# Selective scan: three of sixteen products with C on GpSimd, B's product for both halves at once, step sizes summed by TensorE, B's rows broadcast by DMA

## What is computed

```python
dt = softplus(einsum('btr,ir->bti', dt_lo, dt_proj_w) + dt_proj_b)
def step(h, inp):
    dt_t, B_t, C_t, x_t = inp
    dA = exp(dt_t[..., None] * A[None])
    dBx = dt_t[..., None] * B_t[:, None, :] * x_t[..., None]
    h = dA * h + dBx
    y_t = sum(h * C_t[:, None, :], axis=-1)
...
y = (y + Dp * xc) * silu(z)
return einsum('bti,di->bd', y, out_proj_w)
```

## Time and profile before

| | us |
|---|---|
| median of three runs | 4557.76 |
| the profiled execution | 4557.68 |
| its span, first to last instruction | 4555.9 |
| first scan instruction starts | 1192.81 |
| last product with C starts | 2063.63 |
| last copy of the stage (`take_sum`) starts | 2070.63 |

### The profile page before, as it was taken

How to read it: one execution, slowest core, us unless ns; L and a number is a source line. 1 busy time by engine, 2 the same in 40 slices (tenths; PEclk the granted TensorE clock), 3 DMA queues, 4 the chain that set the end, 5 groups by cost and what they waited for, 6 DMA issues and landing times. The chain is left out here.

```text
span 4555.9 us, 92840 instructions
## 1 busy us (share of the span) xinstructions
PE 3902.2 (86%) x30083; PEld 1984.7 (44%) x30084; DVE 3239.7 (71%) x7596; ACT 2951.3 (65%) x5997; POOL 2373.4 (52%) x2953
## 2 busy tenths in 40 slices
PE   7599999899677777779879999996988699997897
PEld 4244444463222222226423333335984244443896
DVE  3588888448799999994459999982116688887013
ACT  7488888767666666666758888883334477775332
POOL 3266666211688899980321545454544336665452
PEclk9799999999899999999979999998998799998997
DMA  9533333004310000000263333334655534442666
GB/s 279 166 90 86 86 87 88 23 0 162 110 40 34 29 29 29 29 15 0 103 200 88 91 88 90 89 83 138 211 191 194 173 107 118 115 113 81 198 215 197
DMA packets 500325, 486.05 MB, mean 107 GB/s; under 512 B 160194, under 2 KB 434755, under 8 KB 499808
## 3 DMA queue, kind: packets, MB, share of 16 engines
q1 hardware_dynamic: 481744, 443.29, 32.4%
q0 software_dynamic: 18160, 37.42, 2.3%
HBM read 321.07 MB, written 159.42 MB: 105 GB/s over the span
## 5 line engine op out<-in xcount | busy, mean ns | idle before, releaser
L1668 ACT ACTIVATE p_probs<-p_t_ps 128x512 f32<-128x512 f32 (+1 forms) x2048 | 1028.9, 557 | 345.8 <-PE p_t_ps L1427 149.4
L1448 PE MATMUL p_o_ps<-p_probs,p_v_st 128*32 128x256 f32 (+3 forms) x9728 | 749.8, 381 | 10.8 <-ACT p_o_sb L1630 10.1
L1761 DVE TENSOR_REDUCE p_row_max<-p_s_ps 128x1 f32<-128x512 f32 x1024 | 632.8, 678 | 56.2 <-PE p_s_ps L1376 56.1
L2449 POOL TENSOR_TENSOR p_dbx<-p_dtx,p_b_sb 128x512 f32<-128x512 f32 x512 | 635.7, 1274 | 42.8 <-DVE p_state L2498 40.0
L1376 PE MATMUL p_s_ps<-p_s_k,p_s_q 48*128 48x512 bf16 (+3 forms) x3072 | 607.0, 335 | 49.0 <-DVE p_row_max L1758 35.1
L2498 DVE TENSOR_TENSOR_SCAN p_state<-p_da,p_dbx 128x1024 f32<-128x1024 f32 x256 | 584.7, 2284 | 21.0 <-issue 18.1
L1409 PE MATMUL p_t_ps<-p_t_q,p_t_k 50*128 50x512 bf16 (+3 forms) x3072 | 545.2, 333 | 50.1 <-DMA p_t_q<-shifts 20.0
L1758 DVE CUSTOM_DVE_ANT_0 p_tried<-p_s_ps,c_mask_row 128x512 bf16<-128x512 f32 (+3 forms) x1024 | 441.2, 485 | 85.4 <-PE p_s_ps L1376 78.0
L1758 DVE CUSTOM_DVE_ANT_0 p_tried<-p_s_ps,p_s_bias 128x512 bf16<-128x512 f32 (+3 forms) x1024 | 441.6, 481 | 82.1 <-PE p_s_ps L1376 80.4
L1312 POOL TENSOR_TENSOR p_probs<-p_probs,xn 128x384 f32<-128x384 f32 (+1 forms) x384 | 408.8, 1092 | 153.9 <-ACT p_probs L1666 153.6
L2271 PE MATMUL p_y_ps<-p_prod,c_ident 128*128 128x512 f32 x1024 | 484.4, 595 | 3.4 <-DVE p_gated L2515 3.4
(11 more groups left out here) (308 smaller groups left out, 7205.3 us busy)
## 6 DMA issues: line engine op xcount, KB each, us to landing
p_wb<-in_w SPq DMA_DIRECT2D x142, 512.0 KB, 3.6
p_s_q<-stack_q SPq DMA_DIRECT2D x384, 96.0 KB, 2.3
p_s_k<-stack_k SPq DMA_DIRECT2D x384, 96.0 KB, 2.4
p_t_q<-stack_q SPq DMA_DIRECT2D x384, 96.0 KB
p_t_k<-stack_k SPq DMA_DIRECT2D x384, 96.0 KB
mamba_inputs<-p_out SPq DMA_DIRECT2D x16, 1536.0 KB, 5.6
p_raw<-routed_rows SPq DMA_DIRECT2D x142, 130.0 KB, 3.1
stack_q<-p_parts SPq DMA_DIRECT2D x48, 384.0 KB, 2.8
```

Of the source, the lines that this page charges most:

```text
L1448: mm = pe.matmul(o_ps[32 * j:32 * j + 32, at:to], v_st[:, g % 2, c, j, :], probs[:, g % 2, j, place[c] + at - first:place[c] + to - first] ...
L1668: act.activation(exps, tile, ACT.Exp, scale=scale).then_inc(expd, 1)
L1761: read = dve.tensor_reduce(found, scores, X, ALU.max)
L2449: pool.tensor_tensor(dbx[:, n % R, half(h)], dtx[:, u, h], b_sb[:, n % RB], ALU.mult).then_inc(dbx_ready, 1)
```

## The change

`mamba_in`: C's rows are split into three bf16 parts as before (16 rows in place of 32), and the rows of C and B are also stored as fp32 (one more store for each block, 64 KB). `dbl` gets three buffers in place of one.

`mamba_scan`:
- B's rows no longer pass through PE and ACT. SP loads four rows at a time, broadcast to all partitions (`load_b`, 1024 KB, four for each block, two quads of buffers).
- POOL's product with B is one instruction of 128 x 1024.
- For n = 1, 6 and 11 POOL makes the product with C too, from rows that SP loads broadcast (`load_c`, three of 256 KB), at its steps n = 5, 10 and 15. DVE makes the other 13. PE sums POOL's products at its steps 4, 9 and 14.
- dt is summed by PE: four fp32 matmuls by the identity for each half (`step_sum`, at n = 5 and 7) into a PSUM tile shared with `outward`, and an ACT copy (`take_step`, at n = 9 and 11). POOL's three additions go. ACT's six instructions move to n = 0 to 6, `outward` to n = 3, `take_sum` to n = 7.
- There are eight slots of `state` in place of four. `c_sb`, `gated` and `dbx` lie in the room of `xn`.

```diff
+                buffer_stored(dve, n)
+                if n >= OB:
+                    dve.wait_ge(dt_mm, 2 * (n - OB) + 2)
+                dve.tensor_copy(dbl[:, n % OB], dbl_ps[0:BC + RANK, :]).then_inc(dbl_copied, 1)
...
+                    sp.dma_start(c_dram[n, r], part[:, u]).then_inc(stored[u], 16)
+                sp.dma_start(rows_dram[n], dbl[0:BC, u]).then_inc(stored[u], 16)
...
-    RS = 4
+    RS = 8
     RP = 2
     RA = 2
-    RB = 8
-    AHEAD = 6
-    COPIED = 4
-    AT = 4
+    QUAD = 4
+    RB = 2 * QUAD
     SKIP_AT = (9, 11)
-    OUT_AT = 4
+    OUT_AT, TAKEN_AT = 3, 7
+    DT_AT, DT_COPIED_AT = (5, 7), (9, 11)
+    SCALED_AT = (13, 15)
+    BY_POOL = (1, 6, 11)
+    POOL_BEHIND, POOL_SUM_BEHIND = 4, 3
+    BY_DVE = [n for n in range(STATE) if n not in BY_POOL]
+    D, K = len(BY_DVE), len(BY_POOL)
...
+            def load_steps(b):
+                if b >= 2:
+                    sp.wait_ge(above_ready, 2 * (b - 1))
+                sp.dma_start(inp[:, b % 2, 4:6], mamba_dram[b, 4:6].rearrange("k p t -> p k t")
+                             ).then_inc(step_loaded[b % 2], 16)
...
+            def load_c(b):
+                if b >= 1:
+                    sp.wait_ge(pool_prod_ready, K * b)
+                for j, n in enumerate(BY_POOL):
+                    sp.dma_start(c_sb[:, j], rows_dram[b, n:n + 1].to_broadcast([P, T])).then_inc(c_loaded, 16)
+
+            def load_b(b, q):
+                no = STATE // QUAD * b + q
+                if no >= 2:
+                    sp.wait_ge(dbx_ready, QUAD * (no - 1))
+                at = STATE + QUAD * q
+                sp.dma_start(b_sb[:, QUAD * (q % 2):QUAD * (q % 2) + QUAD].rearrange("p n t -> p (n t)"),
+                             rows_dram[b, at:at + QUAD].rearrange("n t -> (n t)").unsqueeze(0).to_broadcast([P, QUAD * T])
+                             ).then_inc(b_loaded[q % 2], 16)
+
+            load_steps(0)
+            load_steps(1)
+            load_inputs(0)
+            load_b(0, 0)
+            load_b(0, 1)
...
+            load_c(0)
+            load_inputs(1)
+            for b in range(NB):
+                if 1 <= b and b + 1 < NB:
+                    load_steps(b + 1)
+                load_b(b, 2)
+                if 1 <= b and b + 1 < NB:
+                    load_inputs(b + 1)
+                load_b(b, 3)
+                if b + 1 < NB:
+                    load_b(b + 1, 0)
+                    load_b(b + 1, 1)
+                    load_c(b + 1)
...
+            def step_sum(b, h):
+
+                pe.wait_ge(back, 4 * b + 2 * h + 2)
+                pe.wait_ge(soft, 1 + 6 * b + 3 * h + 3)
+                pe.wait_ge(above_ready, 2 * b + h + 1)
+                terms = (lost, small, log1, above)
+                for k, term in enumerate(terms):
+                    mm = pe.matmul(shared_ps[:, :], w["ident"], term[:, h], start=(k == 0), stop=(k == len(terms) - 1))
+                mm.then_inc(dt_mm, 1)
...
+                    if n in BY_DVE:
+                        next_c(b, u, n, last)
+                        sums(b, u, n, first)
+                    if n - POOL_SUM_BEHIND in BY_POOL:
+                        pool_sums(b, u, n - POOL_SUM_BEHIND)
                     if n in SKIP_AT:
                         h = SKIP_AT.index(n)
                         pe.matmul(y_ps[:, h], skip_w[:, h], inp[:, u, h], start=False, stop=False)
                     if n == OUT_AT and not first:
                         outward(b - 1)
-
+                    if n in DT_AT and not last:
+                        h = DT_AT.index(n)
+                        if h == 0 and not first:
+                            pe.wait_ge(added, b + 1)
+                        if h == 1:
+                            pe.wait_ge(dt_ready, 2 * (b + 1) + 1)
+                        step_sum(b + 1, h)
...
+            def take_step(b, u, h):
+                act.wait_ge(dt_mm, 2 * b + h + 1)
+                act.activation(dt[:, u, h], shared_ps[:, :], ACT.Copy).then_inc(dt_ready, 1)
...
-                    if n == OUT_AT + 4 and not first:
+                    if n == TAKEN_AT and not first:
                         take_sum(b - 1)
-                    if n == OUT_AT + 4:
-                        copy_b(b, n - 1 + COPIED)
-                    if n != OUT_AT + 3:
-                        if n + COPIED < STATE:
-                            copy_b(b, n + COPIED)
-                        elif not last:
-                            copy_b(b + 1, n + COPIED - STATE)
...
+                    if n in DT_COPIED_AT:
+                        take_step(b + 1, 1 - u, DT_COPIED_AT.index(n))
...
+            def times_b(b, u, n):
+                q = n // QUAD
+                if n % QUAD == 0:
+                    pool.wait_ge(b_loaded[q % 2], 16 * (STATE // QUAD // 2 * b + q // 2) + 16)
+                pool.wait_ge(scanned, STATE * b + n + 1)
+                if n == 0:
+                    pool.wait_ge(dtx_ready, 2 * b + 2)
+                pool.tensor_tensor(by_half(dbx[:, n % R]), dtx[:, u],
+                                   b_sb[:, n % RB].unsqueeze(1).to_broadcast([P, 2, T]), ALU.mult
+                                   ).then_inc(dbx_ready, 1)
+
+            def times_c(b, u, n):
+                no = K * b + BY_POOL.index(n)
+                if n == BY_POOL[0]:
+                    pool.wait_ge(c_loaded, 16 * K * b + 16 * K)
+                pool.wait_ge(scanned, R + STATE * b + n + 1)
+                pool.wait_ge(pool_acc_mm, 2 * no + 2)
+                pool.tensor_tensor(by_half(pool_prod[:, pool_slot(u, n)]), by_half(state[:, n % RS]),
+                                   c_sb[:, BY_POOL.index(n)].unsqueeze(1).to_broadcast([P, 2, T]), ALU.mult
+                                   ).then_inc(pool_prod_ready, 1)
 
             def sequence(b, u, last=False):
                 for n in range(STATE):
...
+                    times_b(b, u, n)
+                    if n - POOL_BEHIND in BY_POOL:
+                        times_c(b, u, n - POOL_BEHIND)
+                    if n in SCALED_AT and not last:
+                        scale_input(b + 1, 1 - u, SCALED_AT.index(n))
...
+            def state_free(b, n, first):
+
+                back, of = (n - RS) % STATE, b if n >= RS else b - 1
+                if n < RS and first:
+                    return
+                if back in BY_POOL:
+                    dve.wait_ge(pool_prod_ready, K * of + BY_POOL.index(back) + 1)
+                else:
+                    dve.wait_ge(prod_ready, 1 + D * of + BY_DVE.index(back) + 1)
...
-                    scan(b, n)
-                    if n:
-                        times_c(b, n - 1)
-                    elif not first:
-                        times_c(b - 1, STATE - 1)
+                    scan(b, n, first)
+                    if n == 0 and not first:
+                        times_c(b - 1, 1 - u, STATE - 1)
+                    if n and n - 1 in BY_DVE:
```

More of the change, by code:

```diff
@@ L2064, in high_of @@
                 act.wait_ge(dbl_copied, n + 1)
-                act.activation(high[:, n % OB], dbl_ps[0:BC, :], ACT.Copy).then_inc(high_ready, 1)
+                act.activation(high[:, n % OB], dbl_ps[0:STATE, :], ACT.Copy).then_inc(high_ready, 1)
             def middle_of(n):
@@ L2210, in half, with by_half, prod_slot, pool_slot @@
             return slice(h * T, h * T + T)
+        def by_half(tile):
+            return tile.rearrange("p (h t) -> p h t", h=2)
+        def prod_slot(u, n):
+            return (D * u + BY_DVE.index(n)) % RP
+        def pool_slot(u, n):
+            return (K * u + BY_POOL.index(n)) % 2
         @block.sync
         def _(sp):
[L2214 to L2219, removed]
@@ L2249, in broadcast_c @@
             def broadcast_c(b, u, n):
                 if n == 0:
[L2251 to L2256, removed]
+                    inputs_loaded(pe, b, u)
+                pe.wait_ge(prod_ready, 1 + D * b + BY_DVE.index(n))
+                pe.matmul(c_ps[:, :], w["select"][:, n], bc[:, u], start=True, stop=True).then_inc(c_mm, 1)
@@ L2258, in outward, with next_c @@
+            def next_c(b, u, n, last):
+                d = BY_DVE.index(n) + 1
+                if d < D:
+                    broadcast_c(b, u, BY_DVE[d])
+                elif not last:
+                    broadcast_c(b + 1, 1 - u, BY_DVE[0])
+            def outward(b):
                 pe.wait_ge(gated_ready, 2 + 2 * b + 2)
-                pe.wait_ge(added, b + 1)
-                pe.wait_ge(b_ready, 1 + (STATE * (b + 1) + OUT_AT + AHEAD + 1 if follows else STATE * (b + 1)))
+                if isinstance(b, int) and b == NB - 1:
+                    pe.wait_ge(added, b + 1)
+                else:
+                    pe.wait_ge(dt_ready, 2 * (b + 1) + 2)
@@ L2261, in outward @@
                 for h in range(2):
[L2262 to L2267, removed]
+                    pe.matmul(shared_ps[:, :], w["out_w"][:, h], gated[:, h], start=(h == 0), stop=False)
```

(29 more changed lines are left out.)

186 lines of the change are left out of this document (73 added, 113 removed).

## The result

The changed kernel takes 4575.64 us (median of 7 runs, 4569.09 to 4580.24) against 4559.65 for the kernel before on the same chip (7 runs, 4554.76 to 4564.11): a ratio of 1.0034, 95% interval 1.0025 to 1.0044. It is slower by 16 us, where 4535 and faster was forecast. The profiled execution has a span of 4571.7 us, 15.8 more than before.

The account below looks back on a forecast made before the run. DVE's list was taken to bound the scan. From 4557.7 us: -56.8 (products) + 24.4 (waits on PE) + 7.2 (start) + 1.7 (end) + 0.5 (`mamba_in`) = -23.0, so 4535 us; own range 4524 to 4548, wider range 4508 to 4562.

Parts of the forecast that it names:

- DVE's list: In the scan, DVE sheds three products a block: 50.9 us in place of 54.45, 56.8 less for 16 blocks.
- POOL: In the scan, 128x1024 instructions at 2.36 us, 47.4 us a block; POOL stays under DVE and causes no wait.
- the rival with POOL as the bound: In the scan, POOL instructions at 3.0 us need 60.2 us a block, 4659 us in all; chance 0.06.
- ACT and the step loads: At the next block's `magnitude`, the step load lands in time: no wait taken, 0 to 15 us kept.
- the rival of late loads: Step loads at 200 GB/s land late, 1.9 us a block, 4562 us; chance 0.18, over 4540 to 4590.
- The start, the end, `mamba_in`: Outside the loop: first scan 27.4 us after the first load (7.2 more), end 1.7 more, `mamba_in` 0.5 more.
- PE's part: In the scan, PE busy 41.6 of 50.9 us; its late C row 9 holds DVE 1.7 us a block, 24.4 in all.
- the 0.12 for slower: Chance that the whole kernel gets slower: 0.06 POOL as the bound, 0.05 late loads, 0.01 the rest.
- the mechanism of the forecast: At product 9, two step sums on PE delay C row 9, so DVE waits 1.7 us in most blocks.
- the gain of the products: Three products leave DVE in each block of the scan, 3.55 us less a block, 56.8 for 16 blocks.

Follow-up runs that it names:

- e6: The changed kernel with `outward` moved to state 0 and the second step sum to state 8, copied at 12; 4523.16 us, ratio 0.9918.
- e1: The changed kernel plus four fp32 matmuls a block that nobody reads, behind the sums of state 0; 4558.11 us.
- e4: The changed kernel with GpSimd making the products of states 2, 6 and 11 in place of 1, 6 and 11; 4588.79 us, ratio 1.006.
- e3: The changed kernel with all 16 products with C left on DVE and no C rows loaded for GpSimd; 4611.88 us, ratio 1.0113.

## Why the prediction was wrong

**DVE's list** was right: 50.9 us a block, shown by e6. A scan behind a scan is recorded as 4.46 us for two, so 2.2 as taken. The pace before was read a little low: of the two blocks behind the 54.45 the first has no wait, and the steady ones are 54.60 us apart, which makes 2 us in all.

**POOL** was right. 256 products with B and 48 with C (engine, shapes, count | busy, mean ns of one | idle):

```profile
L2485 POOL TENSOR_TENSOR xn<-p_dtx,p_b_sb 128x1024 f32<-128x1024 f32 x256 | 599.8, 2358 | 122.8 <-DVE p_state L2543 119.3 <-POOL p_dtx L2476 0.7
...
L2495 POOL TENSOR_TENSOR p_pool_prod<-p_state,xn 128x1024 f32<-128x1024 f32 x48 | 112.8, 2350 | 0.0
```

The line through the earlier trace rows gave 2.36. DVE waits for POOL at the start of the stage alone, so the rival with POOL as the bound did not come about.

**ACT and the step loads** were right. ACT waits at Abs for the load, 21.6 us in 14 blocks, 2.6 at the longest, and no scan of DVE waits for that; the rival of late loads has no part in the loss.

**The start, the end, `mamba_in`**: 28.1 us after the first load for 27.4, 1.9 for 1.7, 0.8 for 0.5. The two step sums at the start took 4.9 and 5.2 us for the 5.3 taken.

**PE's part is the step that failed**, and in it two things. In the loop 37.0 us are missing (871.5 for 834.5 forecast).

*The clock*, 17.7 of them (e1's loop, from 1203.83 to 2057.59, is 853.8). The step priced every matmul of the loop at the full clock, because the earlier trace rows show 1.00. The list before had a row of B and a product of DVE in every state. The change takes every row of B and three of the products away, and the step counted the matmuls that leave as a relief. The low clock was read and used for the start, but the question was not put to the loop, and PE's list was followed from product 3 on, behind the thin stretch, so that its 4.1 us of idle never came in sight. No rival had it, and the 0.12 for slower stood on mechanisms that had no part.
The Trainium skill (TensorE: Matmul & The Clock Gate, HAM oscillation — how this bites in real kernels) describes a loop whose clock falls in each turn's wait and is paid for in the next turn; here the trace agrees, with 0.50 granted and 3.78 us for 1.98 in the block shown.

*The price of a C row*, nearly all of the other 19.3. At the full clock (e1) a block takes 53.94 us, where the sum has 50.9 + 1.7 = 52.6: 1.34 more, 18.8 in 14 blocks. The step took 0.22 us for a row of C and 1.72 for the sums of a state from the earlier trace rows, whose row at 1379.57 has these neighbours:

```profile
1378.71 1.02 PE L2263 MATMUL p_b_ps<-x,c_ident 128*128 x2
...
1379.79 1.88 PE L2271 MATMUL p_y_ps<-p_prod,c_ident 128*128 128x512 f32 x4
1381.50 0.38 PE L2247 MATMUL p_b_ps<-p_bc,xn 96*128 96x512 bf16 x1
```

Two recorded matmuls of 0.43 from 1378.71 end where that row starts. In the changed kernel row 5 stands between the same two, `outward` and sums. There 0.09 us pass ahead of it (1549.20 + 0.86 = 1550.06) and the sums start 0.32 after it (1550.15 to 1550.47), 0.41 in all. The sums take 1.82 until the next matmul (1550.47 to 1552.29), and product 5 starts 0.52 after its row (1550.67), where 0.39 was taken. Rows 4, 5, 7, 8 and 9 and the sums of states 3, 4, 5 and 7 stand on the path to product 9: 0.9 and 0.4 us, 1.3 of the 1.34. They also make row 8 late, which the step had in time by 0.3 us. The price read was that of the matmul before, over 96 rows; the change makes it one over 48. Whether that is the reason was not tried.

So the mechanism of the forecast, a wait where two step sums crowd C row 9, was there; it was mis-sized by 1.3 us a block, and beside it stood one that it did not know. With the waits mostly got round by placement (e6) the time is 38 us below the kernel before, where 23 were forecast: the gain of the products was real all along.

## What to carry to other kernels

When a change takes small work off TensorE, list its idle stretches after the change and ask where the clock will be when the next crowded stretch begins; matmuls that leave can cost more than they free. Move work that has to be done anyway into the thin stretch (41 us here for one constant), rather than cut the list where it is already thin. And where one PSUM tile hands rows to the bounding engine, price every instruction ahead of such a row in its new surroundings, since a few tenths of a microsecond each were half of this error.

## What was not expected of the hardware

- The clock falls in a loop in which PE is busy 171 of 200 us. It falls with idles of 4.11 us, with 1.86 and 2.1 to 2.6 (every second block of e4), and with none above 1.93 in most blocks of e3. Four fp32 matmuls a block that nobody reads made the kernel 17.5 us faster.
- Between `outward` and sums a bf16 row of C costs TensorE 0.41 us as a matmul over 48 rows, 0.22 over 96 in the kernel before, with neighbours of the same kind. Whether the 48 rows are the reason was not tried and stays open.
